# A fused graph-attention and GNN kernel: the values' bias added by VectorE instead of by a matmul

## The reference, cut to what matters

```python
h = jnp.maximum(_layernorm(x, axis=-1), 0.0)
q = (h @ Wq.T).reshape(b, n, NUM_HEADS, HEAD)
k = (h @ Wk.T).reshape(b, n, NUM_HEADS, HEAD)
v = (h @ Wv.T + bv).reshape(b, n, NUM_HEADS, HEAD)
...
out = jnp.einsum('bhqk,bkhd->bqhd', p, v).reshape(b, n, h)
return out @ Wo.T + bo
```

## Time and profile before

| | before |
|---|---|
| median of 3 runs | 1526.22 us (1525.73 to 1530.09) |
| profiled execution, whole | 1526.11 us |
| its span, first to last instruction | 1524.4 us |
| PE busy | 1454.8 us (95%), 14528 matmuls |
| DVE busy | 1217.8 us (80%), 4559 instructions |
| ACT busy | 897.9 us (59%), 2027 instructions |
| POOL busy | 504.8 us (33%), 926 instructions |
| mean granted TensorE clock | 0.978 of full |
| DMA | 89.18 MB, mean 59 GB/s |

### The profile page before, as it was taken

One profiled execution on the slowest core, in us unless ns is written; L12 is line 12 of the kernel. 1 busy time (PEld: TensorE's weight loads), 2 busy tenths in 40 slices (PEclk: granted clock), 3 DMA queues, 4 the chain that ended last, 5 costly groups with the idle time before them and its releaser, 6 DMA issues.

```text
span 1524.4 us, 40191 instructions
## 1 busy us (share of the span) xinstructions
PE 1454.8 (95%) x14528; PEld 1419.3 (93%) x14528; DVE 1217.8 (80%) x4559; ACT 897.9 (59%) x2027; POOL 504.8 (33%) x926
## 2 busy tenths in 40 slices
PE   4699999999999999999999999999999999999884
PEld 4599999999999999999999999999999999999873
DVE  5578888888888888888888888888888888888753
ACT  4556665556666556666555666655566665566531
POOL 4113433233334233343323333333333342333322
PEclk9799999999999999999999999999999999999896
DMA  6232222222221223222222232122332322223200
GB/s 209 53 57 57 67 42 59 48 64 67 57 62 42 57 57 64 59 65 48 55 50 60 67 57 67 42 57 50 64 67 57 54 49 54 58 65 57 53 11 11
DMA packets 235682, 89.18 MB, mean 59 GB/s; under 512 B 206832, under 2 KB 235248, under 8 KB 235488
## 3 DMA queue, kind: packets, MB, share of 16 engines
q1 hardware_dynamic: 234912, 85.63, 26.8%
q0 software_dynamic: 576, 0.99, 0.3%
HBM read 23.66 MB, written 12.58 MB: 24 GB/s over the span
## 4 chain that ended last, share of the span: by engine, by line
PE 93%; DVE 2%; ACT 1%; DMA 1%; issue 1%; POOL 1%; SPq 0%; DVEq 0%; POOLq 0%; ACTq 0%
PE bank L342 81%; PE bank L348 4%; PE bank L419 4%; PE bank L407 2%; PE bank L426 1%; DMA pT<-prob_parts 1%; DMA pT<-w 1%; PE bank L438 0%; ACT prob L507 0%; SPq L323 0%; DMA x_sb<-x 0%; DVE weights L570 0%; ACT prob_parts L515 0%; ACT work L556 0%; ACT weights L478 0%
## 5 line engine op out<-in xcount | busy, mean ns | idle before, releaser
L342 PE MATMUL bank<-h,weights 128*128 128x256 f32 x3456 | 431.5, 282 | 2.9 <-DVE h L749 2.9
L342 PEld LDWEIGHTS bank<-h,weights 128*128 128x128 f32 x3456 | 418.1, 190 | 3.7 <-issue 3.6
L507 ACT ACTIVATE prob<-prob,rmin 128x128 f32<-128x128 f32 x768 | 244.0, 392 | 4.3 <-DVE rmin L664 4.3
L342 PE MATMUL bank<-weights,h 128*128 128x384 f32 x1152 | 227.8, 342 | 0.0
L342 PE MATMUL bank<-hA,weights 128*128 128x256 f32 x1728 | 220.4, 284 | 1.4 <-DVE hA L594 1.4
L485 ACT ACTIVATE n<-bank 128x512 fp32r<-128x512 f32 x192 | 114.2, 595 | 182.1 <-PE bank L342 181.0
L342 PEld LDWEIGHTS bank<-hA,weights 128*128 128x128 f32 x1728 | 213.3, 191 | 1.7 <-DVE hA L594 1.7
L342 PEld LDWEIGHTS bank<-weights,h 128*128 128x128 f32 x1152 | 194.6, 188 | 6.3
L594 DVE TENSOR_TENSOR n<-bank,n 128x512 fp32r<-128x512 f32 x192 | 129.1, 686 | 58.6 <-ACT n L485 58.1
L808 POOL TENSOR_SCALAR less_mean_gnn<-mv_gnn 128x2 f32<-128x2 f32 x64 | 32.8, 513 | 428.1 <-DVE mv_gnn L599 428.1
L664 DVE CUSTOM_DVE_ANT_0 prob<-bank,adj_sb 128x128 f32<-128x128 f32 x768 | 170.9, 287 | 0.1
(11 more groups left out here) (109 smaller groups left out, 2455.8 us busy)
## 6 DMA issues: line engine op xcount, KB each, us to landing
x_sb<-x SPq DMA_DIRECT2D x32, 384.0 KB, 3.2
out<-x SPq DMA_DIRECT2D x32, 384.0 KB, 2.7
adj_sb<-adj SPq DMA_DIRECT2D x32, 128.0 KB, 2.1
pT<-prob_parts SPq DMA_TRANSPOSE x256, 2.8
x<-w SPq DMA_DIRECT2D x3, 576.0 KB, 4.7
pT<-w SPq DMA_DIRECT2D x3, 576.0 KB, 6.0
prob<-w SPq DMA_DIRECT2D x2, 576.0 KB, 8.0
prob_parts<-w SPq DMA_DIRECT2D x2, 576.0 KB, 6.3
```

The costliest lines, as they stand in the source:

```text
L342: mm = pe.matmul(out, lhsT, rhs, start=(n == 0), stop=(n == len(pairs) - 1))
L507: e = act.activation(prob[:, a * C + h // HC, :], prob[:, a * C + h // HC, :], ACT.Exp, bias=rmin[:, j, h:h + 1], scale=-1.0)
```

## The change

V0 and V1 are nine matmuls without the bias. VectorE gets two new steps, va0 and va1, which add `bv_all` (the bias in all 128 partitions, loaded by a broadcast DMA) to the bank, write the sum to the new SBUF tensor `v_sum` and free the bank. ScalarE's V0 and V1 now copy `v_sum` into the high part after va, and VectorE's V0 and V1 make the low part from `v_sum` and the high part. They have semaphores of their own (`s_vhi`, `s_vlo`) in place of the shared one. PV waits for `s_vlo`. In VectorE's list va0 stands between ln2_ag and N10, va1 between N10 and ln1_st, all else is in the old order. `bias_rows`, `pick` and what builds them are gone; VectorE's `make_constants` is one cast, and the wait on `s_const` is now ahead of the first C. va0 of the first pair waits for all the constant loads.

```diff
     "DVE": [
         ("QK2", 1), ("HTb.h", -1), ("HTa.h", -1), ("HTb.l", -1), ("HTa.l", -1), ("WO1", 0), ("ln2_st", 0), ("ln2_ag", 0),
-        ("N10", -1), ("ln1_st", 2), ("N11", -1), ("ln1_ag", 2), ("V0", 1), ("N12", -1), ("HL10", -1), ("V1", 1), ("T2b", 0),
+        ("va0", 1), ("N10", -1), ("va1", 1), ("ln1_st", 2), ("N11", -1), ("ln1_ag", 2), ("V0", 1), ("N12", -1), ("HL10", -1),
+        ("V1", 1), ("T2b", 0), ("T2a", 0), ("U1.m", -1), ("U1.w", -1), ("S01", 1), ("U1.d", -1), ("U1.dh", -1), ("HL11", -1),
...
-                    rows(step, g, WV, hA, int(step[1]), bias=True)
+                    rows(step, g, WV, hA, int(step[1]))
...
-                    wait_drained(pe, f"V{j}", g)
+                    pe.wait_ge(s_vlo[j], g + 1)
...
-                    hi(step, g, v2[:, HI, j, :, 0:D], H, "p (h d) -> p h d", h=NH)
+                    wait_filled(act, f"PV{j}", g - 1)
+                    wait_drained(act, step, g)
+                    act.activation(v2[:, HI, j, :, 0:D], v_sum[:, j, :].rearrange("p (h d) -> p h d", h=NH), ACT.Copy).then_inc(s_vhi[j], 1)
...
             def make_constants():
-                dve.wait_ge(s_bias, 32)
                 dve.wait_ge(s_gconst, 2)
-                dve.tensor_copy(bias_rows[:, :], o_sb[:, 0, :]).then_inc(s_setup_dve, 1)
-                dve.wait_ge(s_setup_dve, 1)
-                dve.tensor_tensor(o_sb[32:64, 1, :], o_sb[32:64, 0, :], bias_rows[32:64, :].bitcast(F32), ALU.subtract).then_inc(s_setup_dve, 1)
-                dve.wait_ge(s_setup_dve, 2)
-                dve.tensor_copy(bias_rows[32:64, :], o_sb[32:64, 1, :]).then_inc(s_setup_dve, 1)
-                dve.tensor_copy(pick[:, :], hx_pick).then_inc(s_setup_dve, 1)
-                dve.tensor_copy(hl[:, :, :, H:HL], ones_zeros).then_inc(s_setup_dve, 1)
-                dve.wait_ge(s_setup_dve, 5)
-                dve.engine_nop().then_inc(s_const, 1)
+                dve.tensor_copy(hl[:, :, :, H:HL], ones_zeros).then_inc(s_const, 1)
...
-                    lo(step, g, v2[:, LO, j, :, 0:D], v2[:, HI, j, :, 0:D], H, "p (h d) -> p h d", h=NH)
+                    dve.wait_ge(s_vhi[j], g + 1)
+                    dve.tensor_tensor(v2[:, LO, j, :, 0:D], v_sum[:, j, :].rearrange("p (h d) -> p h d", h=NH), v2[:, HI, j, :, 0:D],
+                                      ALU.subtract).then_inc(s_vlo[j], 1)
+                elif step[:2] == "va":
+                    j = int(step[2])
+                    job = f"V{j}"
+                    if g == 0:
+                        dve.wait_ge(s_cload, 16 * CONST_LOADS)
+                    ge(dve, s_vlo[j], g)
+                    wait_filled(dve, job, g)
+                    dve.tensor_tensor(v_sum[:, j, :], bank(job)[:, 0:H], bv_all[:, :], ALU.add).then_inc(free(job), 1)
...
-                pool.memset(o_sb[:, 0, :], 0.0).then_inc(s_setup, 1)
-                pool.wait_ge(s_setup, 5)
-                for r in (0, 32):
-                    pool.dma_start(o_sb[r:r + 1, 0, :], bias_d[0:1]).then_inc(s_bias, 16)
...
-                for dst, src in ((bl_all[:, 0, :], bias_d[1]), (bl_all[:, 1, :], bias_d[2]), (bo_all[:, :], bo_d), (lna_all[:, :], lna_d[1]), (lnb_all[:, :], lnb_d[1])):
+                for dst, src in ((bv_all[:, :], bias_d[0]), (bl_all[:, 0, :], bias_d[1]), (bl_all[:, 1, :], bias_d[2]), (bo_all[:, :], bo_d), (lna_all[:, :], lna_d[1]), (lnb_all[:, :], lnb_d[1])):
```

More of the change, by code:

```diff
@@ L112 @@
 }
-SPLIT_JOBS = (["T1a", "T1b", "QK0", "QK1", "QK2", "V0", "V1",
+SPLIT_JOBS = (["T1a", "T1b", "QK0", "QK1", "QK2",
               "OT0", "OT1", "T2a", "T2b"] + [f"N{l}{k}" for l in range(L) for k in range(3)] +
               [f"HL{l}{j}" for l in range(L) for j in range(G)])
-CONST_LOADS = 5 + 2 * C
+CONST_LOADS = 6 + 2 * C
 AHEAD = max(ahead for steps in ORDER.values() for _, ahead in steps)
@@ L154, in build @@
         ident = sb("ident", [P, P])
-        bias_rows = sb("bias_rows", [P, H], F32R)
-        pick = sb("pick", [P, P], F32R)
+        bv_all = sb("bv_all", [P, H])
         bl_all = sb("bl_all", [P, L, H])
@@ L168, in build @@
         xn1 = sb("xn1", [P, G, H])
+        v_sum = sb("v_sum", [P, G, H])
         v2 = sb("v2", [P, 2, G, NH, DA], F16)
@@ L207, in build @@
         s_wload = [sem(f"weight_in{i}") for i in range(4)]
-        s_setup, s_setup_dve, s_carrier = sem("setup"), sem("setup_vector"), sem("carrier")
-        s_whi, s_wlo, s_const, s_cload, s_bias, s_gconst = (sem(n) for n in ("w_hi", "w_lo", "consts", "const_load", "bias_load", "gp_consts"))
+        s_setup, s_carrier = sem("setup"), sem("carrier")
+        s_whi, s_wlo, s_const, s_cload, s_gconst = (sem(n) for n in ("w_hi", "w_lo", "consts", "const_load", "gp_consts"))
+        s_vhi, s_vlo = ([sem(f"value_{n}{j}") for j in range(G)] for n in ("hi", "lo"))
         s_xin = [sem("x_in0"), sem("x_in1")]
@@ L237, in build @@
         s_chain = {k: sem(f"pool_chain_{k}") for k in ("ln1", "ln2", "gnn0", "gnn1")}
-        hx_pick = work[:, 0:P]
         ones_zeros = work[:, 3 * P:3 * P + 4 * G].rearrange("p (s g k) -> p s g k", s=2, g=G)
@@ L360, in project, with rows @@
                 mm.then_inc(full(job), 1)
-            def rows(job, g, m, h, j, bias=False):
+            def rows(job, g, m, h, j):
                 need(m, g)
                 pairs = [(h[:, a, c, j * P:(j + 1) * P], W[:, m, b, c, :]) for c in range(C) for a, b in PARTS]
[L365 to L368, removed]
                 split_mm(bank(job)[:, 0:H], pairs).then_inc(full(job), 1)
@@ L460, in run @@
                     l, j = int(step[1]), int(step[2])
+                    if g == 0 and l == 0:
+                        pe.wait_ge(s_const, 1)
                     pe.wait_ge(s_dlo[l], g + 1)
@@ L774, in make_constants @@
                 pool.memset(ones_zeros, 0.0).then_inc(s_setup, 1)
-                pool.memset(hx_pick, 0.0).then_inc(s_setup, 1)
-                pool.wait_ge(s_setup, 9)
+                pool.wait_ge(s_setup, 7)
                 pool.memset(ones_zeros[:, HI, :, 0:1], 1.0).then_inc(s_setup, 1)
[L778 to L782, removed]
+                pool.wait_ge(s_setup, 8)
                 pool.engine_nop().then_inc(s_gconst, 1)
-                for dst, src in ((bl_all[:, 0, :], bias_d[1]), (bl_all[:, 1, :], bias_d[2]), (bo_all[:, :], bo_d), (lna_all[:, :], lna_d[1]), (lnb_all[:, :], lnb_d[1])):
+                for dst, src in ((bv_all[:, :], bias_d[0]), (bl_all[:, 0, :], bias_d[1]), (bl_all[:, 1, :], bias_d[2]), (bo_all[:, :], bo_d), (lna_all[:, :], lna_d[1]), (lnb_all[:, :], lnb_d[1])):
                     pool.dma_start(dst, src.unsqueeze(0).to_broadcast([P, H])).then_inc(s_cload, 16)
```

## The result

The changed kernel took 1507.87 us in the median of 4 runs (1506.59 to 1509.11), beside 1525.97 us of the kernel before (4 runs, 1524.67 to 1530.09). The ratio is 0.9884, with a 95% interval from 0.9866 to 0.9903. The forecast was 1514.8 us with a range down to 1511.8. The direction was right, and the gain is two thirds larger than forecast: by the profiled executions 1526.11 - 1507.34 = 18.8 us instead of 11.3.

What follows compares the result with a forecast made beforehand. PE was taken as the bound, busy in all of the 44.85 us period. Removed matmuls 10.9 us plus start 0.4 us gave 11.3 us off 1526.11, so 1514.8 us, range 1511.8 to 1519.0.

Steps and rivals of the forecast that it cites:

- The removed matmuls: PE, V0 and V1: 62 bias matmuls outside the start, at 0.175 us each, save 10.9 us.
- The adds, the waits and the low parts: DVE and ScalarE, steady state: 1.12 us of adds per pair, later high parts and SBUF-reading low parts cost nothing.
- the second rival: DVE sets the pace between WO1 and U1, exposing 1.12 us of adds per pair: 1549.5 us, chance 0.03.
- What is late next: PE at HTb and N10: both covers of 0.56 us keep about 0.38 us, so no new wait.
- The rival of the thin covers: PE waits at HTb or N10, up to 0.35 us per pair: 1525.7 us, chance 0.04; in part, about 1520, 0.08.
- The third rival: V0's low part and POOL's ln1 chain delay each other, reaching PE through xn1, 0.6 us per pair: 1533.5 us, chance 0.01.
- The start: Setup before the first PV0: less bias work on DVE saves 0.4 us, bounds 0 and 2.3 us.

Runs made afterwards that it cites:

- e3: The changed kernel with one 128x384 matmul put back in V1, its result overwritten: 1515.03 us, ratio 0.993 to the kernel before.
- e1: The kernel before without the tenth (bias) matmul of V0 and V1, nothing moved and the bias not added: 1506.94 us, ratio 0.9878.
- e4: The changed kernel with one 128x384 matmul put back in V0, its result overwritten: 1520.95 us, ratio 0.9968 to the kernel before.
- e5: The kernel before with one short matmul of 32 columns ahead of N10: 1521.83 us, ratio 0.9971.
- e8: The changed kernel with each of VectorE's two adds made twice: 1512.23 us, ratio 0.9915 to the kernel before.
- e2: The kernel before with `pick` allocated behind `carrier` and an unused tensor of `v_sum`'s size behind `xn1`: 1519.33 us, ratio 0.9959.
- e12: The changed kernel run again without any edit: 1507.44 us, ratio 0.9878 to the kernel before.
- e10: The changed kernel with OT0 ahead of QK2 in the written order: 1510.49 us, ratio 0.9909 to the kernel before.
- e6: The changed kernel with a short matmul of 32 columns ahead of QK0: 1510.54 us, ratio 0.9897 to the kernel before.
- e7: The changed kernel with a short matmul of 32 columns ahead of each of QK0, QK2 and N02: 1514.4 us, ratio 0.9927 to the kernel before.

## Why the prediction was right in direction and wrong in size

**The removed matmuls.** The price of 0.175 us each was right: in e3 one such matmul costs 0.17 us, V0's and V1's next jobs start that much earlier, and 62 of them make the forecast 10.9 us. The estimate of 0.1625 us by the Trainium skill (VectorE: DVE Perf Modes, the errata cycle table) stays below the 0.17 measured. The step that failed is the one that went unsaid: that a job which the change does not touch keeps its length. I priced the matmuls that go and took every other row of PE as fixed. N10 to N12 changed by 0.24 us per pair, some 30 x 0.24 = 7.2 us, and V1's nine by 0.03, some 0.9 us. With 10.9 for the matmuls that makes 19.0 us, against the 19.2 between the anchors. That the removal alone brings the 7.2 is shown by e1, and e4 takes it back with one matmul in V0. That it works through the way in which the 54 are entered is shown by e5 and by WO1's distances; what in that entry decides is open.

Could it have been foreseen? The distances of the single matmuls were in the trace of before, 117.8 ns in N10 against 113 and 114 in N00, behind its first two (206 116 114 113 114), so a term for a rhythm that flips could have been in the range: 54 x 4.5 ns = 0.24 us per pair, a further 7 us of gain here, or nothing. N10 to N12 ran in the slower rhythm, so a flip there could only gain; whether it comes could not be told, and still can't.

**The adds, the waits and the low parts** cost nothing, as forecast: e1, without any of them, has the same period. The idle time ahead of N10's low part fell from 0.65 to 729.08 - (728.42 + 0.53) = 0.13 us (about 0.1 forecast). But the count of the cover was wrong in kind. I added four idle times of DVE to 2.22 us as the point at which the second rival decides. The last, 0.42, is no cover for U1, and in e8 DVE still had idle time when ScalarE's queue, late behind the second add, held N12's low part back. About twice the adds' time fitted with 0.13 us per pair coming through, so the conclusion had room, but the engine to watch was ScalarE, which the prediction had priced for the single adds only.

**What is late next.** Nothing: HTb, N10, T2b and U1 start right behind their predecessors, as forecast. The rival of the thin covers did not come. (The third rival's sum is 0.1 us off: 1526.1 + 18.6 - 11.3 = 1533.4.)

**The start** was to give 0.4 us and gave nothing in the two profiled executions: the first PV0 starts at 49.40 us, where it was 49.33. The timelines of DVE, POOL, PE and SP in the start of the kernel after:

```profile
32.40 1.02 DVE L598 BATCH_NORM_STATS2 stats_ln<-x_sb 128x6 f32<-128x384 f32 x2 [3.49 <-DMA x_sb<-x]
...
33.62 0.53 DVE L645 TENSOR_TENSOR v<-v_sum,v 128x384 f16<-128x384 f32 x1
...
33.80 0.44 POOL L787 TENSOR_SCALAR less_mean_ln<-mv_ln 128x2 f32<-128x2 f32 x1 [10.24 <-DVE mv_ln L590]
34.30 1.20 POOL L788 TENSOR_SCALAR spread_ln<-mv_ln 128x2 f32<-128x2 f32 x1
35.58 0.90 POOL L790 TENSOR_TENSOR scale_ln<-spread_ln,minus_half 128x2 f32<-128x2 f32 x1
36.55 0.65 POOL L792 TENSOR_TENSOR shift_ln<-less_mean_ln,scale_ln 128x2 f32<-128x2 f32 x1
...
49.40 1.18 PE L415 MATMUL bank<-v,pT 128*128 128x33 f16 x36 [7.92 <-DMA pT<-prob_parts]
...
25.21 0.49 SPq L304 DMA_DIRECT2D x_sb<-x  x1
```

The first two of the same four POOL instructions in the kernel before, and its first PV0:

```profile
33.67 0.23 POOL L795 TENSOR_SCALAR less_mean_ln<-mv_ln 128x2 f32<-128x2 f32 x1 [6.20 <-DVE mv_ln L599]
33.97 0.22 POOL L796 TENSOR_SCALAR spread_ln<-mv_ln 128x2 f32<-128x2 f32 x1
...
49.33 1.19 PE L419 MATMUL bank<-v,pT 128*128 128x33 f16 x36 [7.99 <-DMA pT<-prob_parts]
```

That the x load bounds the changed start was read rightly from the earlier trace rows. It is issued 1.85 us earlier now, but it takes 7.2 us instead of 5.2 and lands at the same time; DVE waits 3.49 us for it. The 0.33 us wait behind it is gone, and DVE's next work came 0.5 us earlier. But POOL's chain of four ended at 37.20 instead of 35.76. Its first instruction now runs beside V0's low part, which reads two SBUF tensors. Its second, 1.20 us instead of 0.22, runs beside the weight split, which always read two but now starts at 34.06 instead of 34.35, because the wait ahead of it is gone. So xn1 started at 37.24 instead of 36.17 and the first softmax at 38.45 instead of 38.34. I had placed this rival in the steady state, where it cost nothing, and not in the start, where it used up DVE's lead. The sentence of the Trainium skill on this (SBUF — State Buffer, "Who interferes with whom") agrees with these rows: 1.20 us beside two-input work of DVE, against 0.22 beside none.

The other traces show how little one pair of starts can tell. With the old setup PV0 starts at 49.33, 49.32 (e5), 47.84 (e1) and 47.83 (e2); the changed kernel's repeat (e12) has 50.06 instead of 49.40. The time from the second pair's statistics to PV0 is 17.06 us in before and 17.00 to 17.05 in all eleven traces of the changed kernel and its variants (17.26 to 18.17 in e1, e2 and e5), so what differs most is when those statistics start: between 30.50 and 32.27 us in the four traces with the old setup, and between 32.05 and 34.83 in the eight with the new one and the old order of loads, each of them behind a wait of 1.3 to 3.6 us for the x load. The 0.4 us can't be checked against that spread. If anything the new start is later, and why the load lands so late in it stays open.

## What to carry to other kernels

Where one engine is busy without a gap, a removed instruction is worth the distance to the next start, not its duration. That estimate holds for the instruction alone. A long stretch of identical back-to-back matmuls behind it can change its spacing by 4%, so put the matmuls of such stretches times the difference of spacings seen in the trace into the range. Count as cover only the idle time that lies ahead of the waiting engine's job, and follow the queues of the other engines that wait for the added work: here one of those was late first.

## What the runs showed of the hardware that was not expected

Back-to-back matmuls of 256 columns with a weight load each, at the full granted clock, ran at 113.3 or 117.8 ns and kept the one or the other for up to 54 matmuls. The rhythm was changed by leaving out the tenth matmul of V0 and V1 (e1), by one matmul more in V0, with PV1, WO0, transposes, V1 and WO1 between it and N10 (e4), by the places of tensors, the bias matmul's own weights among them (e2), and by one matmul of 27 ns (e5), and it differed between pairs of the same run (e10). The job ahead shows it in its own distances. The first matmul behind transposes or a short matmul takes about 200 ns to the next instead of 113 to 118. What in the chip makes the two rhythms, and which entry leads to which, stays open: e6, e7 and e10 tried to pick the fast one on purpose, and only N02 in e7 took it, at no gain.
